# A graph layer on one core: GpSimd waits for its own row gathers at every sixteenth gather of a block

## The chip, the cores and the metric

One of the cores of a Trainium2 chip runs the whole program. The metric is the device time of one execution in microseconds (us). TensorE does the matrix products, VectorE and ScalarE the elementwise work, GpSimd issues the gathers (indirect DMAs), SyncE issues plain DMAs.

## The reference

Three terms are added up over 6250 nodes of 256 features. A graph neural network sums the neighbours' rows of 100,000 edges, a linear attention mixes all nodes, and then comes the part that matters here, a mixture of experts whose gate is a graph attention (GAT) over 131,072 random edges plus the nodes' self loops:

```
h = (x_flat @ W_gat).reshape(M, HEADS, NUM_EXPERTS)
e = leaky_relu(a_src[src] + a_dst[dst], negative_slope=0.2)
ee = exp(e - e_max[dst]);  denom = segment_sum(ee, dst)
alpha = ee / (denom[dst] + 1e-16)
agg = segment_sum(h[src] * alpha[:, :, None], dst)
scores = layernorm(agg + b_gat) ... mean over the heads
w = softmax(top 2 of the 4 scores)
out = sum over e of g_e * (gelu(x @ W1[e] + b1[e]) @ W2[e] + b2[e])
```

So the attention gives each node the gates of its experts, and the experts themselves depend only on x. Both can go on at the same time, and they meet in the last stage.

## The kernel before

The program is a row of stages, each an `nc.Block()` in which every engine has its own list of instructions and meets the others by semaphores; at the end of a block all engines meet. After the sorting and the first gathers (`prepare`, `aggregate`, whose 784 gathers of 1 KB rows are line 857; there GpSimd waits, four gathers into each half block of eight, until the half block before has landed) and after `gnn_out` comes the stage of this change, `gat_gather_experts` (lines 1656 to 2093). The last stage is `gat_combine` (line 2096 on).

In `gat_gather_experts` two jobs run side by side.

**The experts.** The nodes are 7 groups of 896, and for each group come 4 experts, 28 in all. TensorE does the first layer of an expert in 8 units (line 1996), ScalarE applies the gelu (L2061), TensorE does the second layer in 7 units (L2011), ScalarE copies the result out of PSUM (L2068) and stores 896 KB of it (`y_d`, L2070). An expert is 15 units, all experts are 420.

**The attention.** The edges are sorted by destination and lie in 128 lanes. A gather, line 1821, brings one edge's row for each of the 128 lanes: 128 rows of 24 floats from `hx_d` into column `w` of one of four buffers of `edge_rows`. The first 648 columns are always needed and are cut in 7 blocks, `spans`: five of 112 gathers, one of 56, one of 32. (More blocks follow under an `If` for a wide input; in this input they are not run.) All gathers of a block count on one of two semaphores, `s_rows[j % 2]`, 16 for each gather, and `rows_of[j]` is the count at which block j and all before it on that semaphore have landed. Before a block GpSimd waits for the block two before it to have landed, and from the fourth and fifth block on also for the buffer (L1813 to 1817).

GpSimd is held back by `paced` (L1802): before every second gather k it waits until TensorE has done unit k x 420 / 648 - 7 of the experts, so gathers are spread over the stage and can't run further ahead of the experts than that.

VectorE takes a block with `landed(j)` (L1835, a wait for `rows_of[j]`), then `maxima(j)` (first instruction L1848), then `sums(j)` (L1877 to L1888). Between them ScalarE does the exponentials (L2077); for blocks 0 to 4 it does so just before experts 7, 12, 17, 22 and 27 (`due`), for blocks 5 and 6 after the last expert. Between the blocks VectorE makes one-hot tiles (`ones`, L1935 and L1936) out of which TensorE counts a histogram (L2019) between its expert layers. Before block 5 stands `places()` (L1939 to 1968), which waits for TensorE's last two products of the stage (L2037, L2038), queued behind all experts. SyncE stores each finished block (`summed`), and loads the next group for the experts (`turned`).

In `gat_combine` GpSimd gathers 49 rows of ends of segments (L2175), TensorE carries sums across lanes, VectorE works out the gates and adds the weighted experts, group by group.

Of the kernel before, what the change touches and what calls it, by code (L numbers as in the profile page):

```python
# [1655 lines left out]
def gat_gather_experts(c, a, plan, hot, early, far_in):  # L1656
# [21 lines left out]
    with ctx:  # L1678
        G = sb("edge_rows", [P, RING, BLOCK, ROW])
        s_rows = [c.sem(f"gg_rows{i}") for i in range(2)]  # L1680
        rows_of = [16 * sum(n for _, n in spans[j % 2:j + 1:2]) for j in range(len(spans))]
# [54 lines left out]
        EXPERT_UNITS = NF + NS  # L1736
        LEAD = EXPERT_UNITS // 2
        FEW = 2
        with nc.Block() as block:
            @block.sync  # L1740
            def _(sp):
# [54 lines left out]
            @block.gpsimd  # L1796
            def _(pool):

                pool.indirect_dma_start(first_row[:], None, c.hx_d,
                                        bass.IndirectOffsetOnAxis(ap=plan.first[:], axis=0)).then_inc(s_first, 16)  # L1800

                def paced(k):  # L1802

                    n, u = divmod(k * GROUPS * EXPERTS * EXPERT_UNITS // W_LOW - LEAD, EXPERT_UNITS)
                    if n >= 0 and u < NF:
                        pool.wait_ge(s_f, n * NF + u + 1)
                    elif n >= 0:
                        pool.wait_ge(s_s, n * NS + u - NF + 2)

                def gathers(j):  # L1810
                    at, n = spans[j]
                    if j >= 2:
                        pool.wait_ge(s_rows[j % 2], rows_of[j - 2])  # L1813
                    if j == RING - 1:
                        pool.wait_ge(s_blankst, 16 * BLANKS)
                    if j >= RING:
                        pool.wait_ge(s_st[j % 2], 16 * ((j - RING) // 2 + 1))
                    for w in range(n):
                        if j < LOW_SPANS and w % FEW == 0:
                            paced(at + w)  # L1820
                        pool.indirect_dma_start(G[:, j % RING, w, :], None, c.hx_d,  # L1821
                                                bass.IndirectOffsetOnAxis(ap=plan.idx[:, at + w:at + w + 1], axis=0)).then_inc(s_rows[j % 2], 16)

                for j in range(LOW_SPANS):
                    gathers(j)
                with pool.If(pool.value_load(plan.width[0:1, 0:1], min_val=0, max_val=1) > 0):
                    for j in range(LOW_SPANS, len(spans)):
                        gathers(j)
# [639 lines left out]
def program(nc, a, out):  # L2468
# [29 lines left out]
    with ctx:  # L2498
        hot = sb("lane_hot", [P, TILES, P])
        early = [sb(f"co_rows{i}", [P, EXPERTS + 1, GT, D]) for i in range(2)]  # L2500
        c.s_load = [c.sem(f"co_in{i}") for i in range(NB)]
        far = sb("far_row", [P, ROW]), sb("far_both", [P, TILES, HEADS]), c.sem("far_in")
        gat_gather_experts(c, a, plan, hot, early, far)
        gat_combine(c, a, out, plan, hot, early, far)
# [16 lines left out]
```

## Time and profile before

| | us |
|---|---|
| three timed runs | 2258.86, 2253.89, 2258.68; median 2258.68 |
| span of the profiled execution | 2712.5 |
| of it, stage `gat_gather_experts` | about 1502 to 2524 |
| TensorE busy in the whole span | 1935.5 (71%) |
| GpSimd busy in the whole span | 1474.4 (54%) |
| mean granted TensorE clock | 0.825 |

The span runs from the first to the last instruction of the one profiled execution, and is the only time that is given for it. Each instruction's start and length are from that execution. "Idle before" is the time that an engine stood still before an instruction, and "<-" names what ended it; "issue" means that nothing in the profile held the engine. "remote" is a semaphore whose sender the profile does not name. The bar of 40 digits is the busy share of forty equal slices in tenths. The length of a gather's instruction is GpSimd's work on it; the data moves in DMA packets on queue q0.

### The profile page before, as it was taken

What the parts mean: (1) busy time and instruction counts of PE and PEld (TensorE: products, weight loads), DVE (VectorE), ACT (ScalarE), POOL (GpSimd) and SP (SyncE); (2) the same over time, 40 slices, a digit from 0 to 9 for tenths busy, and PEclk for the clock granted to TensorE, in tenths of its full rate; (3) what the DMA queues carried; (4) which work ended last, traced back from release to release, by engine and by line L of the source; (5) the groups of instructions that cost most, each with busy time, mean ns of one, the idle gap of its engine ahead of it and who ended that gap; (6) DMA issues with size and microseconds to landing.
All of it is one profiled execution on the core that took longest, in us unless ns stands there. A gap on an engine that the chain in (4) does not pass through costs nothing. (4 is left out here: it accounts for less than half of the span.)

```text
span 2712.5 us, 26680 instructions
## 1 busy us (share of the span) xinstructions
PE 1935.5 (71%) x7528; PEld 1334.5 (49%) x7528; DVE 1195.4 (44%) x2204; ACT 893.4 (33%) x1910; POOL 1474.4 (54%) x1512
## 2 busy tenths in 40 slices
PE   5588778876766776666547788878888788884235
PEld 4454445454544544444336455555555565553223
DVE  6353222344454555443348433324424344256368
ACT  3433345444435343443315211321222213132124
POOL 2456456565656665556630566666666666661510
PEclk8888789887888888777775799998999889897555
DMA  5443222234334433435329511121211212215544
GB/s 182 147 132 123 62 82 86 72 117 135 117 112 130 130 118 105 131 93 179 89 61 296 208 36 50 36 70 36 70 36 50 56 45 61 51 36 172 159 148 152
DMA packets 197044, 282.80 MB, mean 104 GB/s; under 512 B 43024, under 2 KB 147443, under 8 KB 195762
## 3 DMA queue, kind: packets, MB, share of 16 engines
q0 software_dynamic: 61280, 115.13, 15.9%
q1 hardware_dynamic: 97218, 121.11, 13.5%
q10 hardware_dynamic: 38416, 44.96, 5.0%
q8 instruction: 66, 1.08, 0.2%
q14 instruction: 64, 0.52, 0.1%
HBM read 195.29 MB, written 85.80 MB: 104 GB/s over the span
## 5 line engine op out<-in xcount | busy, mean ns | idle before, releaser
L857 POOL DMA_INDIRECT ag_msg<-xn_tab,step_src x784 | 782.1, 998 | 504.9 <-issue 224.0
L1821 POOL DMA_INDIRECT edge_rows<-hx_d,gat_src x648 | 621.2, 959 | 329.6 <-issue 187.4
L1125 PE MATMUL ag_ps<-ag_msg,ag_hot 128*128 x1760 | 494.0, 430 | 113.5 <-issue 67.8
L1125 PEld LDWEIGHTS ag_ps<-ag_msg,ag_hot 128*128 128x128 f32 x1760 | 366.8, 216 | 238.5 <-issue 181.2
L879 DVE TENSOR_TENSOR acc<-acc,ag_ps 128x257 f32 x440 | 186.0, 423 | 671.1 <-remote 329.8
L2011 PE MATMUL ex_psY<-co_rows 128*128 128x256 f32 x1568 | 401.4, 413 | 100.2 <-issue 44.5
L2011 PEld LDWEIGHTS ex_psY<-co_rows 128*128 128x128 f32 x1568 | 320.8, 208 | 175.6 <-issue 68.7
L1996 PE MATMUL ex_psF<-co_rows 128*128 128x448 f32 x896 | 360.7, 557 | 42.8 <-ACT co_rows L2061 16.9
L1301 ACT ACTIVATE gat_self<-iota_row,step_nloc 128x128 f32<-128x128 f32 x880 | 271.4, 388 | 343.3 <-issue 199.1
L1935 DVE TENSOR_TENSOR hi_one_low<-hi_numbers,hi_low 128x2048 bf16<-128x2048 f32 x64 | 146.4, 2287 | 481.3 <-remote 309.5
L1996 PEld LDWEIGHTS ex_psF<-co_rows 128*128 128x128 f32 x896 | 172.2, 196 | 214.5 <-issue 187.6
L2061 ACT ACTIVATE co_rows<-ex_psF,ex_b 128x448 f32<-128x448 f32 x224 | 136.1, 633 | 247.6 <-PE ex_psF L1996 166.6
L2068 ACT COPY co_rows<-ex_psY 128x512 f32<-128x512 f32 x112 | 59.3, 532 | 473.2 <-remote 207.3
L1142 PE MATMUL mx_ps<-wqkv,xnT 128*128 128x512 f32 x196 | 105.1, 663 | 55.7 <-ACT gat_dst L1314 40.5
L1303 ACT ACTIVATE ag_hot<-gat_self,ones 128x1024 f32<-128x1024 f32 x110 | 126.3, 1148 | 13.6 <-issue 6.0
L1194 PE MATMUL mx_ps<-wself,xnT 128*128 128x256 f32 x196 | 62.4, 448 | 83.4 <-DVE xnT L903 55.4
L1936 DVE TENSOR_TENSOR hi_one_high<-hi_numbers,hi_high 128x1568 bf16<-128x1568 f32 x64 | 114.0, 1781 | 0.0
L1194 PEld LDWEIGHTS mx_ps<-wself,xnT 128*128 128x128 f32 x196 | 41.2, 219 | 95.7 <-DVE xnT L903 59.1
L1142 PEld LDWEIGHTS mx_ps<-wqkv,xnT 128*128 128x128 f32 x196 | 40.4, 211 | 89.8 <-issue 44.2
L1312 ACT ACTIVATE gat_dst<-mx_ps 128x256 f32<-128x256 f32 x49 | 18.7, 382 | 190.7 <-PE mx_ps L1145 87.9
L218 DVE TENSOR_TENSOR gatsort_keys<-gatsort_keys 128x512 f32<-128x512 f32 x117 | 80.2, 686 | 1.0
L219 DVE TENSOR_TENSOR gatsort_keys<-gatsort_keys 128x512 f32<-128x512 f32 x117 | 80.1, 685 | 0.0
(377 smaller groups left out, 2004.9 us busy)
## 6 DMA issues: line engine op xcount, KB each, us to landing
y_d<-co_rows ACTq DMA_DIRECT2D x28, 896.0 KB
co_rows<-y_d SPq DMA_DIRECT2D x28, 896.0 KB, 9.5
ag_msg<-xn_tab,step_src POOLq DMA_INDIRECT x784
xnT<-base_d SPq DMA_DIRECT2D x7, 1792.0 KB
edge_rows<-hx_d,gat_src POOLq DMA_INDIRECT x648
base_d<-xnT ACTq DMA_DIRECT2D x7, 1024.0 KB
sums_d<-edge_rows SPq DMA_DIRECT2D x5, 1344.0 KB
xg<-in_x_dram SPq DMA_DIRECT2D x7, 896.0 KB, 6.1
```

The lines of the kernel that those rows point to most:

```text
L857: pool.indirect_dma_start(msg[:, q, u, 0:D], None, c.xn_tab, bass.IndirectOffsetOnAxis(ap=t.idx[:, at:at + 1], axis=0)).then_inc(s_g[q], 16)
L879: V.tensor_tensor(own, own, bank[(at // JOIN + u) % BANKS][:, 0:ROWW], ALU.add).then_inc(s_acc, 1)
L1125: last = nc.tensor.matmul(bank[(at + r) % BANKS][:, 0:ROWW], hot[:, k, u0 + r * JOIN + j, :], ring[:, j * ROWW:SLOTS * ROWW][:, ds(places[ ...
L1142: nc.tensor.matmul(b[:, :], xnT[:, k, at:at + P], wqkv[:, k, D:3 * D], start=(k == 0), stop=False, skip_group_check=True)
L1301: A.activation(dif[:, u, :], c.iota_row[:], ACT.Abs, bias=t.nloc[:, ds(half * SHALF + u, 1)])
L1303: A.activation(hot[:, k], dif[:], ACT.Relu, bias=c.ones[:, 0:1], scale=-1.0).then_inc(s_hot, 1)
L1821: pool.indirect_dma_start(G[:, j % RING, w, :], None, c.hx_d, bass.IndirectOffsetOnAxis(ap=plan.idx[:, at + w:at + w + 1], axis=0)).then_i ...
L1935: V.tensor_tensor(one_low[:, k % 2], bcast(numbers, 1, HIST), bcast(low[:, at], 2, P), ALU.is_equal)
L1936: V.tensor_tensor(one_high[:, k % 2], bcast(numbers[:, 0:HIGHS], 1, HIST), bcast(high[:, at], 2, HIGHS), ALU.is_equal).then_inc(s_one, 1)
L1996: last = nc.tensor.matmul(psF[i % FB][:, 0:HB], w1[:, e, k, (i % HC) * P:(i % HC + 1) * P], yT[:, k, (i // HC) * HB:(i // HC + 1) * HB], s ...
L2011: last = nc.tensor.matmul(bank[:, (u - u0) * D:(u - u0 + 1) * D], hh[:, k].rearrange("p a b -> p (a b)")[:, u * P:(u + 1) * P], w2[:, e, k ...
L2061: nc.scalar.activation(hh[:, i % HC, i // HC, :], psF[i % FB][:, 0:HB], ACT.Gelu, bias=b1[:, e * HC + i % HC:e * HC + i % HC + 1]).then_in ...
```

## The change

One constant, and one wait inside the loop that issues the gathers of a block. At w = 16, 32, 48, ... of a block, behind the pacing wait and ahead of gather w, GpSimd waits until all w gathers of this block that it has issued so far have landed.

```diff
         LEAD = EXPERT_UNITS // 2
         FEW = 2
+        RUN = 16
         with nc.Block() as block:
...
                     for w in range(n):
                         if j < LOW_SPANS and w % FEW == 0:
                             paced(at + w)
+                        if w and w % RUN == 0:
+
+                            pool.wait_ge(s_rows[j % 2], rows_of[j] - 16 * (n - w))
                         pool.indirect_dma_start(G[:, j % RING, w, :], None, c.hx_d,
                                                 bass.IndirectOffsetOnAxis(ap=plan.idx[:, at + w:at + w + 1], axis=0)).then_inc(s_rows[j % 2], 16)
```

## Rows read from the trace of the kernel before

**Rows 1.** The page's head: span, then busy time, share and count by engine.
```profile
span 2712.5 us, 26680 instructions
PE 1935.5 (71%) x7528; PEld 1334.5 (49%) x7528; DVE 1195.4 (44%) x2204; ACT 893.4 (33%) x1910; POOL 1474.4 (54%) x1512
```
**Rows 2.** Chain that ended last, last stage: start us, us, what (its earliest pieces).
```profile
2524.36 0.05 issue
2524.41 0.15 DVE gc_pen L2270
```
**Rows 3.** Busy time by stretch: stretch, length, each engine's busy us, clock, DMA share, GB/s.
```profile
1500.00:2465.00 965.00, 806.44 (x3492) 545.79 (x3492) 360.22 (x349) 225.76 (x362) 622.14 (x649) 0.91 0.22 60
```
**Rows 4.** TensorE, end of experts: start us, us, engine, line, out<-in, count, idle.
```profile
2453.68 10.59 PE L2011 MATMUL ex_psY<-co_rows 128*128 128x256 f32 x40 [3.24 <-ACT co_rows L2061]
2464.26 0.39 PE L2038 MATMUL hi_ps<-hi_counts,ones 128*128 128x49 f32 x2
```
**Rows 5.** VectorE in order of time: first read of block 0, 4, 5 and 6.
```profile
1710.86 1.27 DVE L1848 TENSOR_TENSOR gs_own<-edge_rows,gat_self 128x448 f32<-128x448 f32 x1
...
2415.68 1.27 DVE L1848 TENSOR_TENSOR gs_own<-edge_rows,gat_self 128x448 f32<-128x448 f32 x1
...
2490.88 0.71 DVE L1848 TENSOR_TENSOR gs_own<-edge_rows,gat_self 128x224 f32<-128x224 f32 x1
...
2509.47 0.47 DVE L1848 TENSOR_TENSOR gs_own<-edge_rows,gat_self 128x128 f32<-128x128 f32 x1
```
**Rows 6.** GpSimd in order: gather 0, last of block 0, first of block 1, last of 4, 5, 6.
```profile
1503.82 0.98 POOL L1821 DMA_INDIRECT edge_rows<-hx_d,gat_src  x1 [0.30 <-issue]
...
1663.55 0.94 POOL L1821 DMA_INDIRECT edge_rows<-hx_d,gat_src  x1 [0.30 <-issue]
1664.80 0.94 POOL L1821 DMA_INDIRECT edge_rows<-hx_d,gat_src  x1 [0.30 <-issue]
...
2325.60 0.94 POOL L1821 DMA_INDIRECT edge_rows<-hx_d,gat_src  x1 [0.30 <-issue]
...
2409.41 0.94 POOL L1821 DMA_INDIRECT edge_rows<-hx_d,gat_src  x1 [0.30 <-issue]
...
2453.33 0.94 POOL L1821 DMA_INDIRECT edge_rows<-hx_d,gat_src  x1 [0.31 <-issue]
```
**Rows 7.** GpSimd's waits, 1500 to 2465: us in total, times, longest us.
```profile
POOL edge_rows L1821 <- issue: 187.4, 579, 2.7
POOL edge_rows L1821 <- remote: 82.4, 33, 4.0
POOL edge_rows L1821 <- PE ex_psF L1996: 42.1, 24, 4.6
POOL edge_rows L1821 <- PE ex_psY L2011: 17.6, 12, 4.9
```
**Rows 8.** DMA between 2455 and 2456 us: bar of 40 slices, queue with packets, MB, share.
```profile
DMA  1120389000000000000000000000000000000000
q0 software_dynamic: 28, 0.01, 7.6%
```
**Rows 9.** DMA between 2402 and 2410 us, with an expert's store: bar and queues; the page's row of the stores.
```profile
DMA  0600000410999999999999983910000000000003
q10 hardware_dynamic: 912, 0.92, 34.4%
q0 software_dynamic: 157, 0.06, 8.2%
...
y_d<-co_rows ACTq DMA_DIRECT2D x28, 896.0 KB
```
**Rows 10.** GpSimd around that store, in order of time.
```profile
2404.31 0.94 POOL L1821 DMA_INDIRECT edge_rows<-hx_d,gat_src  x1 [0.30 <-issue]
2408.16 0.94 POOL L1821 DMA_INDIRECT edge_rows<-hx_d,gat_src  x1 [2.90 <-remote]
```
**Rows 11.** GpSimd in the first gather stage: longest wait for its own rows.
```profile
1094.48 1.85 POOL L857 DMA_INDIRECT ag_msg<-xn_tab,step_src  x1 [3.54 <-DMA ag_msg<-xn_tab,step_src]
```
**Rows 12.** TensorE's waits, 1500 to 2465, that end with nothing named.
```profile
PE ex_psY L2011 <- issue: 44.5, 49, 7.5
PE hi_ps L2019 <- issue: 16.3, 17, 2.5
PE ex_psF L1996 <- issue: 12.5, 14, 2.5
```

## The prediction

> **What bounds the kernel now.** I read the page's head first [rows 1]: TensorE is busiest, GpSimd second, and neither is full, so shares decide nothing. The chain of waits that ended last goes back to 2524.36 us, the start of the last stage, and holds no gather of the changed line [rows 2]. So the question is what ends the stage before it, and by how much the changed gathers could come later without moving that end.
>
> The busy table for 1500 to 2465 us shows TensorE busy 806.44 of 965 us at a granted clock of 0.91, GpSimd 622.14, VectorE 360.22, DMA 22% [rows 3]. TensorE leads. Its last expert product ends at 2464.27, and behind it its two small products release VectorE at 2464.65 [rows 4]. From there VectorE does `places()`, takes block 5 at 2490.88 and block 6 at 2509.47 [rows 5], and block 6 ends the stage. In this chain the gathers appear only through `landed(j)`. Compare GpSimd's last gather of a block with VectorE's first read of it [rows 5, 6]: block 0 is issued by 1664.49 and read at 1710.86, 46 us later; block 4 2326.54 and 2415.68, 89 us; block 5 2410.35 and 2490.88, 81 us; block 6 2454.27 and 2509.47, 55.2 us. Blocks 1 to 3 lie between. VectorE is held by its order of work each time, never by rows, and the gathers are not on the path. What would make them count is 55 us of delay at block 6, or more at the others.
>
> **How many waits.** A block of 112 gets them at w = 16 to 96, six; five such blocks give 30, the block of 56 three, the block of 32 one: 34. Blocks behind the `If` are not run. The target, `rows_of[j] - 16 (n - w)`, is exactly the count of everything issued on that semaphore so far, because block j - 2 was already waited for. So each wait empties GpSimd's gathers in flight.
>
> **What one wait costs GpSimd.** Between two plain gathers GpSimd idles 0.30 us, whether or not a pacing wait stands there that is already met [rows 6], so a met wait is free. An unmet one costs the landing time behind the end of the issuing instruction, minus that 0.30. The landing: the last gather of the stage ends its instruction at 2454.27, and its packets are over in the seventh of the forty slices of 2455 to 2456, so at 2455.18, 0.91 us later [rows 6, 8]. That the semaphore counts a little after the last packet no row shows; I add 0.2 us as an estimate, and take 1.1 us. Price: 1.1 - 0.30 = 0.8 us, times 34 = 27 us.
>
> The bounds of this price: below, 0, where the pacing wait just ahead of the new one has itself held GpSimd for over a microsecond, since then all rows are there. Above: a gather may fall into an expert's store. In the stretch 2402 to 2410 the store's packets fill the DMA to about 2407.2 (slice 26 of 40), and a gather whose instruction ended at 2405.25 can be over by then only, 2 us after [rows 9, 10]. There are 28 such stores [rows 9]; at some 3.3 us each they cover a tenth of the stage, 3 or 4 of 34 waits, at 1 us more apiece some 4 us. The farthest row is the first stage's: there a wait for rows cost 3.54 us at worst, for gathers ten times as large [rows 11]. 34 x 3.54 = 120 us is the upper end, and 27 is taken, since the gather of rows 8 is of this very line.
>
> The Trainium skill (DMA: Bandwidth & Descriptors, section Anatomy of one DMA) speaks against so small a price: a DMA whose descriptors GpSimd writes has a fixed cost of about 2.0 us, most of it a write receipt that comes behind the last byte. If all of it lay behind the instruction, the waits would cost 34 x (2.0 - 0.30) = 58 us; no row here shows the receipt, and in the profiled execution those 58 us too would vanish in the next paragraph.
>
> **What hides it.** First the pacing. GpSimd stood 82.4 + 42.1 + 17.6 = 142.1 us for TensorE's units in 69 waits [rows 7], about 5.1 us for each of 28 experts. An expert sees 34/28 = 1.2 new waits, 1.0 us, and by the upper end 4.3 us. A delayed GpSimd is simply stopped for less time at the next pacing wait; it never falls further behind than one or two waits. At the very end the single wait of block 6 (w = 16, 16 gathers before its end) can push the last gather by 0.8 us if no pacing stop follows, up to 3.5. Second the 55.2 us between issue and read, less the landing: 54. If all pacing were gone, 27 us still fits in it. Nobody else waits for these gathers: behind the waiting instruction on GpSimd stand only further gathers of this stage; SyncE's block stores and ScalarE's exponentials hang on VectorE, which reads on time; the buffer waits of later blocks are older than before, not newer. No DMA is added or moved past another queue. The gathers of the last stage start when all engines have met, at 2524, as before.
>
> **Sum.** 27 us more of waiting on GpSimd, 27 hidden, 0 on the path: the span stays 2712.5. The runs have a median of 2258.68, 453.8 below the span, so the profiled execution is much slower than the timed ones. I carry the 0 over: 2259.
>
> **The weak point is that carrying over.** GpSimd's issue without its stops is 2454.27 - 1503.82 - 142.1 = 808.4 us. TensorE's experts took 2464.65 - 1503.82 = 960.8 us in the profiled run. Were the stage shorter in proportion of the whole (2258.68 / 2712.5 = 0.833), TensorE would need 800 us, with GpSimd's pace, if that stays, just above it. All 1481 gathers of the kernel at 0.94 + 0.30 = 1.25 us make 1850 of the 2259 us. So it is possible that in the timed runs pacing hides nothing. Then the second cover counts alone. GpSimd ends at 808 + 27 + 1 = 836 us, and VectorE wants block 6 at TensorE's end plus 44.8 (2509.47 - 2464.65). It is late if TensorE's experts take under 791 us. What speaks against so short a stage: TensorE's busy 806.44 us at clock 0.91 is 734 at full clock, and even with only half of its 158 us of idle time that makes 813.
>
> **Rivals.**
> - *GpSimd binds, slower.* The place is block 6, the price is what the gathers' end exceeds TensorE's end plus 45 us. At 791 us it begins, below 764 the whole 27 us are paid: 2259 + 27 = 2286; with the 4 us of stores 2290, and if every wait took the 2 us of rows 9 and 10 (1.7 x 34 = 58) 2317. For it: the proportion gives 800, only 9 us away. Against it: the instruction times of GpSimd should shrink in that proportion too, and the clock sum. Chance 0.15.
> - *Calmer traffic, faster.* TensorE stood 44.5 + 16.3 + 12.5 = 73.3 us in this stage with nothing named [rows 12]. If bunches of gathers in flight slowed its instruction supply, emptying them might give some back. GpSimd is silent for only 27 us more out of 950, 3%, and by rows 8 it is so that before the change, too, hardly more than one gather is in flight; 3% of 73.3 is 2 us, and a tenth, 7 us, would need far more than that: 2252. Chance 0.09.
> - *The wait is idle.* If rows have always landed when GpSimd reaches it, nothing changes: 2259. By rows 8 it isn't so, as 0.30 is less than 0.91, but the time is that of the forecast. Chance 0.05, counted with it.
>
> **How the numbers follow.** The forecast, waits that are real and hidden, has 0.71, the idle wait 0.05, the binding GpSimd 0.15, calmer traffic 0.09. What a measurement of this kernel can tell from no change is about 0.3%, 6.8 us. Same: 0.76, faster 0.09, slower 0.15. The three runs spread over 5 us, so the forecast's own range is 2252 to 2264. The range that should hold 8 in 10 takes a bit below it and reaches up to the first rival's 2286, rounded to 2285, low end 2251.
>
> **What would show it in the profile after.** GpSimd: 34 idle pieces of 1.0 to 1.3 us (a few of 2) before gathers of L1821, named as a DMA into `edge_rows`, less those that fall on a pacing stop, and the pacing stops down from 142 us to about 115. The last gather of the stage stays within 3 us of 11 us ahead of TensorE's end. VectorE's first reads of the seven blocks show no idle time before them that ends with a DMA. If a wait costs over 2 us on average, the price was wrong; if VectorE waits for rows at block 5 or 6, the first rival holds; if the profile shows all of it hidden and the runs are still slower by over 7 us, then the timed runs have less cover than the profiled one.

## The result, and the profile after

The changed kernel takes 2335.62 us (median of 4, 2330.08 to 2343.93) against 2257.23 us before (median of 4): a ratio of 1.0361, interval 1.0338 to 1.0384, 3.6% or 78 us slower. The prediction said 2259 and a range of 2251 to 2285.

One thing has to be said first, since no number can be understood without it. The experiments come from five chips, which the runs number. On chips 11, 3 and 1 the kernel before takes about 2254 us; on chips 13 and 0 it takes 2694 us. I call these the 2254 kind and the 2694 kind. Each of them was used for one set of runs only, so whether the kind is the chip's or the hour's isn't known. The result and its timed runs, whose chip isn't recorded, are of the 2254 kind; the profile that the prediction was read from, with its span of 2712.5 us and its granted clock of 0.825, looks like the 2694 kind. So I took the profile of the kernel before again (e1_before, 2256.94 us, chip 11); it is the one to compare with. A time is compared below only with the kernel before on the same chip. The ratios leave out executions that were slow by themselves on a chip of either kind, such as one of e13's four, 2794.92 us at a granted clock of 0.63.

The heads of the pages of the kernel after and of e1_before, the unchanged kernel:

```profile
span 2336.9 us, 26714 instructions
PE 1809.5 (77%) x7528; PEld 1289.0 (55%) x7528; DVE 1197.4 (51%) x2204; ACT 895.5 (38%) x1910; POOL 1496.1 (64%) x1512
```
```profile
span 2255.1 us, 26680 instructions
PE 1798.3 (80%) x7528; PEld 1281.9 (57%) x7528; DVE 1197.1 (53%) x2204; ACT 895.5 (40%) x1910; POOL 1495.9 (66%) x1512
```

Busy time hardly moved; 82 us of waiting came in. Where, is seen in GpSimd's order of time. First the kernel after: first gather, a stop, last gather.

```profile
1243.49 0.98 POOL L1825 DMA_INDIRECT edge_rows<-hx_d,gat_src  x1 [0.30 <-issue]
...
2140.61 0.94 POOL L1825 DMA_INDIRECT edge_rows<-hx_d,gat_src  x1 [0.31 <-issue]
2143.70 0.94 POOL L1825 DMA_INDIRECT edge_rows<-hx_d,gat_src  x1 [2.15 <-DMA edge_rows<-hx_d,gat_src]
...
2162.42 0.95 POOL L1825 DMA_INDIRECT edge_rows<-hx_d,gat_src  x1 [0.30 <-issue]
```

Then e1_before, with the pause that stands at the second gather of a block there:

```profile
1245.15 0.98 POOL L1821 DMA_INDIRECT edge_rows<-hx_d,gat_src  x1 [0.30 <-issue]
...
1386.15 0.94 POOL L1821 DMA_INDIRECT edge_rows<-hx_d,gat_src  x1 [0.30 <-issue]
1390.79 0.94 POOL L1821 DMA_INDIRECT edge_rows<-hx_d,gat_src  x1 [3.69 <-issue]
...
2080.36 0.94 POOL L1821 DMA_INDIRECT edge_rows<-hx_d,gat_src  x1 [0.30 <-issue]
```

From the first gather's start to the last one's (the "row of gathers" below), 835.2 us became 918.9: 83.7 us more. From the last gather's start to the end of the program it is 174.7 us before and 174.5 after. The whole difference lies inside the row of gathers, and the rest of the kernel follows it stiffly.

GpSimd's waits in the stage, kernel after (us in total, times, longest), then e1_before:

```profile
POOL edge_rows L1825 <- issue: 196.1, 592, 5.9
POOL edge_rows L1825 <- DMA edge_rows<-hx_d,gat_src: 68.4, 26, 5.6
POOL edge_rows L1825 <- PE ex_psF L2000: 13.2, 19, 2.2
POOL edge_rows L1825 <- PE ex_psY L2015: 12.7, 11, 4.1
```
```profile
POOL edge_rows L1821 <- issue: 200.7, 623, 3.7
POOL edge_rows L1821 <- PE ex_psF L1996: 4.3, 14, 0.3
POOL edge_rows L1821 <- PE ex_psY L2011: 3.4, 11, 0.3
```

Compare with [rows 7]: the 142 us of pacing stops are not there. What e1_before names as a wait for TensorE is at most 0.3 us long, the usual gap. GpSimd issues without a break, 648 gathers in a row, but for five pauses, at the second gather of blocks 1 to 5. In the kernel after, the 34 stops idle for 93 us together. The profile puts 26 of them down to the DMA, seven to TensorE and one to nothing; all 34 stand at the gathers w = 16, 32, ... of a block. Less the 0.30 that each gap has anyhow, that is 83 us: the 83.7.

VectorE's first reads of blocks 4, 5 and 6 stand against [rows 5] so, first after, then e1_before:

```profile
2032.98 1.27 DVE L1852 TENSOR_TENSOR gs_own<-edge_rows,gat_self 128x448 f32<-128x448 f32 x1 [35.36 <-DMA edge_rows<-hx_d,gat_src]
...
2118.93 0.71 DVE L1852 TENSOR_TENSOR gs_own<-edge_rows,gat_self 128x224 f32<-128x224 f32 x1 [24.57 <-DMA edge_rows<-hx_d,gat_src]
...
2164.82 0.47 DVE L1852 TENSOR_TENSOR gs_own<-edge_rows,gat_self 128x128 f32<-128x128 f32 x1 [32.57 <-DMA edge_rows<-hx_d,gat_src]
```
```profile
1963.79 1.27 DVE L1848 TENSOR_TENSOR gs_own<-edge_rows,gat_self 128x448 f32<-128x448 f32 x1 [20.95 <-DMA edge_rows<-hx_d,gat_src]
...
2038.71 0.71 DVE L1848 TENSOR_TENSOR gs_own<-edge_rows,gat_self 128x224 f32<-128x224 f32 x1 [13.55 <-DMA edge_rows<-hx_d,gat_src]
...
2082.68 0.47 DVE L1848 TENSOR_TENSOR gs_own<-edge_rows,gat_self 128x128 f32<-128x128 f32 x1 [30.65 <-DMA edge_rows<-hx_d,gat_src]
```

VectorE waits for rows already before the change. Block 6 is read 2.3 us after the last gather's start, not 56 us. The experts' side, by stretch, ends in e1_before 753.9 us after the first gather (compare [rows 3]); below it the kernel after:

```profile
1245.00:1999.00 754.00, 729.88 (x3492) 515.48 (x3492) 358.59 (x348) 230.14 (x362) 564.63 (x586) 0.99 0.29 75
```
```profile
1243.00:2068.00 825.00, 734.76 (x3492) 517.45 (x3492) 359.21 (x348) 230.23 (x362) 563.75 (x584) 0.94 0.26 69
```

TensorE is busy 97% of its stretch in e1_before at a granted clock of 0.99, and finishes 82 us ahead of the gathers. After the change its wait for ScalarE's gelu in `co_rows` grows, here e1_before, then the kernel after:

```profile
PE ex_psF L1996 <- ACT co_rows L2061: 16.9, 5, 10.5
```
```profile
PE ex_psF L2000 <- ACT co_rows L2065: 80.6, 5, 26.8
```

A likely reading is that late blocks hold up ScalarE's exponentials, and these its gelus. It looks like a cost, but TensorE still ends 95 us ahead of the gathers and isn't on the path.

### The profile page after: what moved, and what is told of

Same layout as the page of the kernel before. It is cut to its first block and busy times, and to the rows that moved or that the text cites. A ratio compares the mean times of both kernels' runs of the same rounds, so it can differ in the third digit from the quotient of the medians.

```text
span 2336.9 us, 26714 instructions
## 1 busy us (share of the span) xinstructions
PE 1809.5 (77%) x7528; PEld 1289.0 (55%) x7528; DVE 1197.4 (51%) x2204; ACT 895.5 (38%) x1910; POOL 1496.1 (64%) x1512
## 5 line engine op out<-in xcount | busy, mean ns | idle before, releaser
L857 POOL DMA_INDIRECT ag_msg<-xn_tab,step_src x784 | 790.7, 1009 | 244.1 <-issue 217.3
L1825 POOL DMA_INDIRECT edge_rows<-hx_d,gat_src x648 | 629.8, 972 | 290.4 <-issue 196.1
L2000 PE MATMUL ex_psF<-co_rows 128*128 128x448 f32 x896 | 352.8, 552 | 94.8 <-ACT co_rows L2065 80.6
L2015 PE MATMUL ex_psY<-co_rows 128*128 128x256 f32 x1568 | 344.2, 380 | 0.0
L2015 PEld LDWEIGHTS ex_psY<-co_rows 128*128 128x128 f32 x1568 | 296.5, 190 | 42.8 <-issue 3.7
L1939 DVE TENSOR_TENSOR hi_one_low<-hi_numbers,hi_low 128x2048 bf16<-128x2048 f32 x64 | 146.3, 2286 | 287.6 <-PE hi_ps L2023 287.5
L1852 DVE TENSOR_TENSOR gs_own<-edge_rows,gat_self 128x448 f32<-128x448 f32 (+2 forms) x7 | 7.5, 1076 | 177.6 <-DMA edge_rows<-hx_d,gat_src 177.5
L1142 PE MATMUL mx_ps<-wqkv,xnT 128*128 128x512 f32 x196 | 93.8, 601 | 0.0
L2081 ACT ACTIVATE gs_ex<-gs_xs 128x896 f32<-128x896 f32 (+3 forms) x11 | 9.5, 862 | 140.1 <-DVE gs_xs L1872 134.7
L2179 POOL DMA_INDIRECT gc_num<-sums_d,gat_endpos x49 | 50.9, 1038 | 15.2 <-issue 15.2
```

Of the source, the lines that this page charges most:

```text
L857: pool.indirect_dma_start(msg[:, q, u, 0:D], None, c.xn_tab, bass.IndirectOffsetOnAxis(ap=t.idx[:, at:at + 1], axis=0)).then_inc(s_g[q], 16)
L1939: V.tensor_tensor(one_low[:, k % 2], bcast(numbers, 1, HIST), bcast(low[:, at], 2, P), ALU.is_equal)
L2000: last = nc.tensor.matmul(psF[i % FB][:, 0:HB], w1[:, e, k, (i % HC) * P:(i % HC + 1) * P], yT[:, k, (i // HC) * HB:(i // HC + 1) * HB], s ...
L2015: last = nc.tensor.matmul(bank[:, (u - u0) * D:(u - u0 + 1) * D], hh[:, k].rearrange("p a b -> p (a b)")[:, u * P:(u + 1) * P], w2[:, e, k ...
L2179: pool.indirect_dma_start(num[:, t, :], None, c.sums_d, bass.IndirectOffsetOnAxis(ap=plan.endpos[:, t:t + 1], axis=0)).then_inc(s_num[int( ...
```

## The experiments

**e1_before**, the kernel before, unchanged.

> The kernel before, profiled again. Theory A (GpSimd's issue of gathers sets the length of the stage in an undisturbed execution, the first rival of the prediction): the span is near 2257, the stage's gathers take about 648 x 1.25 = 810 us with pacing stops of under 30 us in total instead of 142, and VectorE waits for rows at block 6. Theory B (GpSimd had slack, and the emptying waits disturb the DMA or TensorE in some other way): pacing stops stay near 142 us and VectorE never waits for rows.

2256.94 us. Theory A in each point: no pacing stop over 0.3 us, VectorE waits at blocks 3 to 6. Only the length was a little off, 836 us instead of 810: some gathers take more than 0.94 us (626.8 us busy instead of 609), and the five pauses idle 12.4 us, 11 over the usual gap.

**e2_run32, e3_run8**: the number of stops.

```diff
-        RUN = 16
+        RUN = 32      (e3: RUN = 8)
```

> A stop at every 32nd gather: 16 stops instead of 34. Theory A: the cost goes with the number of stops, 16 / 34 of 78 us = 37 us, 2294. Theory C (only the coincidence of late blocks with ScalarE's due exponentials costs, a threshold): far under 37 us, nearer 10.

> A stop at every 8th gather: 13 in each of five blocks, 6 and 3 in the last two, 74 stops. Theory A: 74 / 34 of 78 us = 170 us, 2427. Theory C: less than in proportion once every due time is missed, or more if missed due times pile up.

2289.94 us, ratio 1.0146 (1.0113 to 1.0178), 37 us as theory A said; and 2454.82 us, 1.0897 (1.0860 to 1.0935), 202 us instead of 170. The row of gathers is 871.1 and 1032.4 us long, 36 and 197 us more than in e1_before. So 16, 34 and 74 stops cost 2.3, 2.3 and 2.7 us each. There is no threshold, and theory C is out. The rise at e3 doesn't lie in the stops: over the usual gap they idle 2.2, 2.4 and 2.4 us each in the three traces. It lies in the gathers themselves, busy for 646.0 us in e3 against 626.8, four of them 5.9 to 6.5 us long; why, isn't shown.

**e4_met**: the same 34 waits, but for a count that is long reached.

```diff
-                            pool.wait_ge(s_rows[j % 2], rows_of[j] - 16 * (n - w))
+                            pool.wait_ge(s_first, 16)
```

> The 34 waits stand where they stood but ask for a count that was reached at the start of the stage. Theory A: the cost is the landing, so this is the time of the kernel before, 2257 within 5. Rival: the wait instruction itself breaks GpSimd's run of gathers, up to 78 us.

2253.53 against 2253.26 us, ratio 0.9994 (0.9978 to 1.0010). A wait that is met is free; only one that is not met costs.

**e5_early, e6_late**: stops in one half of the stage.

```diff
-                        if w and w % RUN == 0:
+                        if w and w % RUN == 0 and j < 3:      (e6: and 3 <= j < LOW_SPANS)
```

> The stops in blocks 0 to 2 only: 18 of the 34. Theory A (GpSimd issues without a break through the whole stage, so a stop anywhere delays the last gather): 18 / 34 of 78 = 41 us, about 2295. Theory D (only the end counts, early delay is made up by the pacing): about 0.

> The stops in blocks 3 to 6 only: 16 of the 34. Theory A: 37 us, about 2291, and with the run before it the two halves add up to 78. Theory D: nearly the whole 78 us.

These two, and the next two, came onto a chip of the 2694 kind (13), where the kernel before takes 2693.81 us: 2720.15, ratio 1.0085 (1.0052 to 1.0119), and 2713.07, 1.0033 (0.9983 to 1.0083). Neither theory was written for that. It is the prediction's case, though, and the 26 us of e5 are clear of noise: about half of what the same 18 stops cost on the 2254 kind (e13 below), and not 0.

**e7_before_unpaced, e8_after_unpaced**: without pacing.

```diff
-                        if j < LOW_SPANS and w % FEW == 0:
+                        if False:
```

> The kernel before without its pacing waits. Theory A: they hold nobody in an undisturbed execution (no pacing stop in the trace of e1_before), so the time is the same within 5 us, 2254. Rival: GpSimd runs ahead in places and the gathers disturb the experts, slower by over 7 us.

> The changed kernel without pacing. Theory A: the stops alone cost the time; at most the few stops that end with a TensorE unit after 4 us instead of 2.2 get shorter, so 0 to 8 us less than the changed kernel, 2324 to 2332. Rival: TensorE, held 80 us in all by late exponentials, holds GpSimd back through pacing and makes up a large part of the 78 us; then 2290 to 2315.

On that chip: 3259.2 us, ratio 1.207 (1.200 to 1.214), and 3222.55, 1.193 (1.184 to 1.202). The direction was e7's rival; a price of this size nobody had named. TensorE's waits of e7 in the stage:

```profile
PE ex_psY L2011 <- issue: 353.8, 53, 43.5
PE ex_psF L1996 <- issue: 133.4, 37, 54.5
PE hi_ps L2019 <- issue: 128.4, 54, 2.6
```

and a piece of its order of time, while GpSimd issues gather upon gather:

```profile
1844.36 0.24 PE L2019 MATMUL hi_ps<-hi_one_high,hi_one_low 128*128 128x98 bf16 x1 [2.56 <-issue]
1847.16 0.24 PE L2019 MATMUL hi_ps<-hi_one_high,hi_one_low 128*128 128x98 bf16 x1 [2.56 <-issue]
1849.99 0.24 PE L2019 MATMUL hi_ps<-hi_one_high,hi_one_low 128*128 128x98 bf16 x1 [2.59 <-issue]
1852.80 0.58 PE L2011 MATMUL ex_psY<-co_rows 128*128 128x256 f32 x1 [2.56 <-issue]
```

TensorE gets one product in 2.8 us and waits for nothing that is named; GpSimd starts a gather every 1.40 us there, its instruction at 1.09 us instead of 0.94. In e8, at 1.25 us a gather, it is 2.8 us too. The same trace has the counter-test. By stretch (columns as in [rows 3]), first with GpSimd issuing, then with GpSimd waiting for a buffer:

```profile
1960.00:2100.00 140.00, 25.41 (x56) 12.31 (x56) 0.00 (x0) 2.13 (x4) 108.95 (x101) 0.54 0.11 15
2140.00:2260.00 120.00, 120.00 (x577) 85.91 (x576) 44.27 (x36) 35.11 (x56) 0.00 (x0) 1.00 0.14 46
```

So on that chip gathers without a pause nearly stop TensorE, and pacing is worth 565 us. A milder form of it was in the profile of before [rows 12], and in that profile's last stage, where no pacing stands, the whole of it. TensorE, while GpSimd issues the 49 gathers of that stage, and once these are over:

```profile
2562.45 0.20 PE L2190 MATMUL gc_ps_in<-gc_carry,lane_hot 128*128 128x25 f32 x1 [2.59 <-issue]
2565.25 0.20 PE L2190 MATMUL gc_ps_in<-gc_carry,lane_hot 128*128 128x25 f32 x1 [2.60 <-issue]
...
2593.95 5.33 PE L2190 MATMUL gc_ps_out<-gc_carry,lane_hot 128*128 128x25 f32 x25 [1.20 <-issue]
```

e8 shows one thing more. With no pacing wait beside them its stops are shorter, 1.67 us at the median against 2.2 in the kernel after and in e9:

```profile
POOL edge_rows L1825 <- DMA edge_rows<-hx_d,gat_src: 58.8, 33, 5.3
```

A pacing wait that is met costs nothing alone, but ahead of a stop that isn't met some 0.5 us stand beside it; why, isn't shown.

**e9_after, e10_lag0, e11_lag1, e12_lag4**: the changed kernel, and the stop moved later. So that GpSimd can ask for 16 given gathers while later ones are in flight, each run of 16 counts on a semaphore of its own: two in turn for each of the old two. (To make room, two semaphores of the last stage are taken over from this one, with their counts moved up; `rows_of` and `landed` count on both. The cut leaves that out.)

```diff
+                        if w >= RUN and w % RUN == 4:      (e10: == 0, e11: == 1)
+                            run = w // RUN - 1
+                            pool.wait_ge(s_rows[j % 2][run % 2], before_it[run % 2] + of_run(16 * (run + 1), run % 2))
...
-                                                bass.IndirectOffsetOnAxis(ap=plan.idx[:, at + w:at + w + 1], axis=0)).then_inc(s_rows[j % 2], 16)
+                                                bass.IndirectOffsetOnAxis(ap=plan.idx[:, at + w:at + w + 1], axis=0)).then_inc(s_rows[j % 2][w // RUN % 2], 16)
```

> The changed kernel again, beside the next three on the same chip. The kernel before takes about 2254 us on some chips and about 2694 on at least one. Where it takes 2254, theory A says 78 us more, 2332, as in the result. Where it takes 2694, TensorE paces GpSimd, and it says at most the sum of the two half changes measured there, 2694 x (1 + 0.0085 + 0.0033) = 2726.

> Each run of 16 gathers counts on a semaphore of its own parity, two for each of the old ones, and the stop stands where it stands in the changed kernel, for the same rows. A control of this form: the time of the changed kernel within 5 us.

> The same, but GpSimd issues one more gather before it stops for the 16 before that one. Theory A: the price of a stop is the 2.15 us from the end of an issue to the next start, less 0.30, and one gather more (1.25 us) is issued inside it, so 1.85 - 1.25 = 0.6 us a stop: a quarter to a third of the cost of the changed kernel, some 25 us where that costs 78. Rival: to stop at all costs (queue, restart), then the full 78.

> The same, four gathers later (20 gathers in flight at most instead of 16). Theory A: the rows have landed long before, all is hidden, the time of the kernel before within 5 us. Rival: to stop costs, the full 78; or the emptying itself costs nothing and the limit of gathers in flight does.

The 2694 kind again, another chip (0; before: 2694.45 us). The changed kernel 2722.98, ratio 1.0119 (1.0043 to 1.0195): some 30 us, near the 32 expected. lag0 2714.07, 1.0070 (1.0028 to 1.0113), 9 us below it, where the control was to lie within 5; the intervals overlap. lag1 2690.98, 0.9949 (0.9906 to 0.9993), a little under the kernel before; lag4 2690.7, 0.9999 (0.9948 to 1.0050). GpSimd's waits in e9_after:

```profile
POOL edge_rows L1825 <- remote: 52.7, 27, 3.3
POOL edge_rows L1825 <- DMA edge_rows<-hx_d,gat_src: 44.0, 17, 5.9
POOL edge_rows L1825 <- PE ex_psF L2000: 29.1, 23, 2.6
POOL edge_rows L1825 <- PE ex_psY L2015: 27.5, 14, 3.5
```

Pacing is alive there beside the stops, as [rows 7] had it: 109 us under TensorE's names and "remote", some of the stops among them, against 142. VectorE never waits for rows in that trace. What got longer is the experts' side: TensorE's last product,

```profile
2441.91 0.39 PE L2042 MATMUL hi_ps<-hi_counts,ones 128*128 128x49 f32 x2
```

ends 983.9 us after the first gather at 1458.45, against 960.8 in the profile of before. How the stops reach TensorE there, single profiles don't settle.

**e13_early, e14_lag1, e15_lag4, e16_before_unpaced**: four of these on a chip of the 2254 kind (3), where the kernel before takes 2253.06 us.

> Stops in blocks 0 to 2 only, 18 of 34. Where the kernel before takes 2254 us, theory A: 18 / 34 of 78 = 41 us more. Theory D (only the end counts): 0. Where it takes 2694: about 20 us more, as before.

> The stop one gather later. Where the kernel before takes 2254 us, theory A: 34 x 0.6 = 20 us, with stores in the way up to 30. Rival (to stop costs in itself): 78. Where it takes 2694: within 15 us of it.

> The stop four gathers later. Where the kernel before takes 2254 us, theory A: within 5 us of it. Rival: 78 us. Where it takes 2694: the same as the kernel before.

> The kernel before without pacing waits. Where the kernel before takes 2254 us, theory A: the same within 5 us, as no pacing stop is in its trace. Rival: gathers that run ahead slow TensorE there too. Where it takes 2694: 3260 again.

e13: 2303.21 us, ratio 1.0222 (1.0171 to 1.0273), 50 us for 18 stops where 41 were expected, the row of gathers 43.5 us longer. A stop in the first half costs no less than the average one; nothing makes it up. e14: 2278.73, 1.0119 (1.0078 to 1.0160), 26 us. e15: 2245.94, 0.9968 (0.9950 to 0.9986). Against the kernel before, one gather issued ahead of the stop takes away two thirds of the price, and four take all. Some of that is the new semaphores' doing: they alone are worth 10 us (e17 below), and against e17 the stops of e14 cost 35 us and those of e15 2. GpSimd's wait for rows in e14, then in e15:

```profile
POOL edge_rows L1829 <- DMA edge_rows<-hx_d,gat_src: 41.7, 34, 4.5
```
```profile
POOL edge_rows L1829 <- DMA edge_rows<-hx_d,gat_src: 8.2, 22, 1.2
```

34 stops of 1.23 us on average in the one, 22 of 0.37 in the other, where 0.30 is the plain gap. The average of e14 comes from ten stops of 1.4 to 4.5 us; 19 of the 34 are under 0.6. They stand at odd gathers, with no pacing wait beside them, so the 0.5 us of e8 may be saved too. e16: 2255.01, 1.0009 (0.9990 to 1.0028). Pacing is idle on this kind of chip; to remove it neither helps nor harms.

**e17_form_only, e18_lag4_again**: e15 was 7 us faster than the kernel before, which nothing had said. On chip 1 (before: 2254.1 us) e17 takes the stop out of e15, and e18 is e15 again.

```diff
-                        if w >= RUN and w % RUN == 4:
+                        if False:
```

> The four semaphores of the lag kernels, and no stop at all. Theory E (the pause at a block's second gather comes with the first use of another semaphore while gathers on the old one are in flight): there would be a pause at every change, 40 instead of 5, some 80 us more. Theory F (the semaphores of their own remove the pauses): the time of e15_lag4, 7 us below the kernel before. Theory G (the late stop removes them): the time of the kernel before, within 4 us, with the five pauses in the trace.

> e15_lag4 again. Where the kernel before takes 2254 us: 2246 within 4, a ratio of 0.995 to 0.999, and no pause at the second gather of a block. Where it takes 2694: the same as the kernel before.

e17: 2243.91, ratio 0.9953 (0.9935 to 0.9971). e18: 2246.35, 0.9964 (0.9950 to 0.9978). Theory F: the semaphores in turn do it, the stop has no part. GpSimd's longest "issue" gap falls from the 3.7 us of e1_before to 0.3 in e17:

```profile
POOL edge_rows L1829 <- issue: 188.7, 619, 0.3
```

The pauses at the second gather of blocks 1 to 5 are gone, and the row of gathers is 821.3 us long, 14 less. It is the fastest version of the study, 0.5% under the kernel before. Why the pauses come with one semaphore for the gathers of a block and go with two in turn is not settled, the less so as they went on the 2254 kind only: e10, e11 and e12, on chip 0, still have pauses of 1.9 us at some blocks' second gather.

## Why the prediction was wrong

**The count and the place of the stops** were right: 34, all real. **The chain** from `places()` over blocks 5 and 6 to the end of the stage was read rightly, and so was the mechanism of the first rival: block 6 is where it bites, and it bites in full once TensorE's experts take less than 764 us. They took 753.9. That rival had a chance of 0.15 and should have been the forecast.

**The step that failed is "I carry the 0 over"**, under "Sum": that what was hidden in an execution of 2712 us would be hidden in those of 2258. It wasn't: the row of gathers is the path there, and the stops came out as time in full, 83 us in the profiles. The 142 us of pacing stops [rows 7] and the 55 us between last gather and read [rows 5, 6] were both real, but on a kind of chip where TensorE gets its instructions late. On the other kind GpSimd has no slack at all: its 648 gathers, 835 us, are the stage. The text had the signs in hand, the 454 us between span and runs, the 808 us of issue without stops against 800 in proportion, and argued them away with two estimates. One was that GpSimd's issue would shrink in the same proportion; it did not (0.94 + 0.30 us a gather on both kinds, and 1.09 in a part of e7). The other was a clock sum that kept half of TensorE's 158 us of idle; e1_before has 24 us of idle in 754. The 808 was too low besides. The 142.1 us taken off [rows 7] include the usual 0.30 of 69 gaps, 20.7 us, which GpSimd idles with or without a stop, so its issue comes to 829 us. Then the first rival begins at 829 + 27 + 1 - 45 = 812 and not at 791, and of the text's own two figures for TensorE 800 lies below it and 813 just above. Added up so, the first rival was no outsider.

**"0 on the path" didn't hold on the 2694 kind either.** There e5 and e9 cost 26 and some 30 us, clear of noise, where the text had 27 hidden in full and even 120 covered. VectorE never waited for rows, as predicted. But TensorE's experts took 983.9 us instead of 960.8 in e9, and the sum had no path from the stops to TensorE. What that path is stays open.

**The price of a stop was mis-sized** besides: 0.8 us of idle time over the usual gap was taken, 2.4 measured. The packets were as predicted. DMA between 2141 and 2144 us in the kernel after, in 40 slices of 75 ns, around the stop shown above:

```profile
DMA  8220000000000000272200000000000000000000
```

The last gather's instruction ends at 2141.55, its packets in slice 20, at 2142.5, so 0.95 us later (0.91 was read from [rows 8]). But the next gather starts at 2143.70, another 1.2 us on, where I had added 0.2. Of the 34 stops 25 are 2.1 to 2.3 us long, nine 2.6 to 5.9 us. In each of the nine, packets of the plain DMA queues q1 or q10 share the DMA engines; in 20 of the 25 short ones there are none. The longest ends at 2085.93; DMA between 2080 and 2086:

```profile
DMA  9999999999999999999999999999999999999999
q1 hardware_dynamic: 1943, 1.96, 107.2%
q0 software_dynamic: 128, 0.05, 3.3%
```

So the 83 us are 34 x 1.9 = 64 for plain landings and 19 for nine that met other traffic, where the text had 27 and 4. The Trainium skill (DMA: Bandwidth & Descriptors, section Anatomy of one DMA) was the better guide: it puts most of a fixed 2 us into a receipt that comes behind the last byte. The trace agrees in size, 2.15 us from the end of the instruction to the next start, 1.2 of them behind the last packet; what share of the 1.2 us is receipt, semaphore or restart, no row separates. Its sum, 58 us, comes near the 64 and leaves out the other traffic. With the right price and the wrong cover the forecast would have been the same 0, which is why the cover is the step that counts. With the right cover and the wrong price it would have been the first rival's 2286, 50 us short.

**Calmer traffic** is no gain here: e13 and e2 cost what their stops cost. On the 2694 kind the stops do take something off when nothing paces (e8 is 37 us below e7), but that is a fraction of what pacing saves.

**Open:** what starves TensorE on the 2694 kind while GpSimd issues, and whether it stays with a chip; how the stops cost time there; why gathers get longer in e3; what the pauses at the block's second gather are. A stop for all but the newest gathers on the old semaphores wasn't tried; the lag kernels stand in its place. The late half of the stops (e6) was measured only on the 2694 kind, and so was the new form with the stop in its old place (e10).

## What to carry to other kernels

Before slack is read from a profile, hold its span against the timed runs: at 20% more it is another state of the machine, and waits and slack in it may be that state's. Here the instruction counts and GpSimd's gap and issue time carried over; the slack did not. On an engine that issues one after the other without a pause, a wait for its own last DMA costs the whole landing, here 2.4 us on average, in the first half of the stage too; ask for an older batch instead, on a semaphore of its own and with four gathers issued behind it, and it costs nothing. Ask of each pacing wait whom it holds: here nobody on the 2254 kind of chip, and on the 2694 kind it is worth a fifth of the time.

## What the runs showed of the hardware that was not expected

- The same kernel takes 2254 us on chips 11, 3 and 1 and 2694 on chips 13 and 0, with a mean granted clock of 0.87 to 0.88 there and 0.83 here. GpSimd's gather instruction takes 0.94 us on both, and 1.09 in the middle of e7.
- On chip 13 TensorE gets one product in 2.8 us while GpSimd issues gathers without a pause, and is busy all of its time when GpSimd waits (e7); unpaced gathers cost 565 us. On chip 3 the same program costs 2 us, within the noise (e16).
- After the last packet of a gather of 128 rows of 96 bytes it takes 1.2 us until GpSimd, waiting for it behind a met pacing wait, starts its next one. Where no pacing wait stands beside, the whole stop is 1.67 us instead of 2.2 (e8 against e9).
- A pause of 1.9 to 3.7 us stands at the second gather of blocks 1 to 5 in e1_before, and is gone on the 2254 kind when each run of 16 gathers counts on its own one of two semaphores in turn: 10 us of 2254 (e17).
